# A Mamba, slot and attention block on one core: ScalarE takes the SiLUs at unit 40 in place of 42, z first, and the opening is laid out anew

## The reference

```
h = layernorm(x); xc, z = split(h @ in_w.T)            # 512 channels each
xc = silu(causal_conv4(xc) + conv_b)
dt, B, C = split(xc @ xp_w.T)                          # 16, 16, 16
dt = softplus(dt @ dtp_w.T + dtp_b)
state = exp(dt * A) * state + dt * xc * B              # 512 x 16 states, a scan over tokens
y = (sum over 16 states of state * C + xc * D) * silu(z)
x = x + y @ out_w.T
```

## Time and profile before

| | us |
|---|---|
| median of 3 runs (lowest to highest) | 2333.46 (2328.74 to 2335.32) |
| the profiled execution | 2333.48 |
| its span in the trace | 2331.7 |
| end of the last VectorE instruction of the Mamba in the trace | 1755.4 |

### The profile page before, as it was taken

The page is one execution under the profiler, slowest core; times in us unless marked ns, Lnnn a source line. Parts: engine busy times, 40 slices in busy tenths (PEclk is TensorE's granted clock), DMA queues, the critical chain, the costliest instruction groups (busy, mean ns, idle before and its releaser), DMA issues. The chain is left out here.

```text
span 2331.7 us, 40782 instructions
## 1 busy us (share of the span) xinstructions
PE 2067.5 (89%) x14787; PEld 1241.9 (53%) x14787; DVE 1880.3 (81%) x2584; ACT 1795.9 (77%) x3062; POOL 1654.9 (71%) x1448
## 2 busy tenths in 40 slices
PE   5989898998989898989989898989874879999987
PEld 2445455454545455554545454554533557777765
DVE  6788889898988889898988888888988656666655
ACT  3988998989898988989888989989864434455453
POOL 2789889898989889898989898898995253223110
PEclk9999999999999999999999999999996889999998
DMA  7340505142341515142331405041415000000012
GB/s 243 72 114 23 128 13 124 47 100 67 70 108 29 123 54 128 38 117 56 82 96 41 114 23 128 19 118 40 107 55 179 1 10 20 11 15 16 11 40 73
DMA packets 112237, 166.45 MB, mean 71 GB/s; under 512 B 13219, under 2 KB 58531, under 8 KB 111653
## 3 DMA queue, kind: packets, MB, share of 16 engines
q1 hardware_dynamic: 112036, 163.86, 26.8%
HBM read 125.53 MB, written 34.08 MB: 68 GB/s over the span
## 5 line engine op out<-in xcount | busy, mean ns | idle before, releaser
L640 POOL TENSOR_TENSOR h<-h,C_rep 128x512 f32<-128x512 f32 x1021 | 1270.5, 1277 | 196.3 <-ACT h_carry L549 196.3
L415 DVE TENSOR_TENSOR_SCAN h<-decay,h_carry,psum 128x512 f32<-128x512 f32 x768 | 955.7, 1270 | 126.5 <-PE psum L771 93.8
L541 ACT ACTIVATE decay<-dt_rep,A 128x512 f32<-128x512 f32 x1024 | 729.4, 713 | 96.6 <-DVE h L415 93.3
L771 PE MATMUL psum<-ident,u_B 128*128 128x128 f32 x2048 | 322.0, 282 | 125.1 <-DVE h L415 98.2
L771 PEld LDWEIGHTS psum<-ident,u_B 128*128 128x128 f32 x2048 | 235.2, 141 | 310.4 <-DVE h L415 215.2
L771 PEld LDWEIGHTS psum<-ident,k_r 128*128 128x128 f32 x2048 | 243.3, 142 | 248.8 <-issue 124.7
L415 DVE TENSOR_TENSOR_SCAN h<-decay,zero,psum 128x512 f32<-128x512 f32 x256 | 318.8, 1271 | 50.2 <-PE psum L771 34.7
L771 PE MATMUL psum<-ident,k_r 128*128 128x128 f32 x2048 | 309.9, 279 | 14.2 <-DVE h L415 9.0
L563 ACT ACTIVATE u_B<-u_tok,B_tok 128x512 f32<-128x512 f32 x416 | 295.1, 709 | 35.3 <-PE psum L771 35.3
L563 ACT ACTIVATE k_r<-u_tok,B_tok 128x512 f32<-128x512 f32 x416 | 294.4, 710 | 28.9 <-DVE u_tok L385 17.7
L784 PE MATMUL psum<-h,state_sum 128*32 128x512 f32 x2048 | 279.8, 619 | 3.6 <-POOL h L640 3.4
(11 more groups left out here) (238 smaller groups left out, 2877.2 us busy)
## 6 DMA issues: line engine op xcount, KB each, us to landing
dt_rep<-dt_rows SPq DMA_DIRECT2D x256, 256.0 KB, 5.5
C_rep<-C_rows SPq DMA_DIRECT2D x256, 64.0 KB, 2.0
dt_rows<-x_dt_gated SPq DMA_DIRECT2D x32, 512.0 KB, 4.9
residual<-mamba_residual SPq DMA_DIRECT2D x16, 512.0 KB, 4.0
mamba_residual<-residual SPq DMA_DIRECT2D x16, 512.0 KB, 2.9
x_tok<-mamba_residual SPq DMA_DIRECT2D x15, 512.0 KB, 4.4
f_gru_weights<-in_slot_gru_dram SPq DMA_DIRECT2D x2, 2176.0 KB
u_B<-in_x_dram SPq DMA_DIRECT2D x8, 512.0 KB, 9.1
```

The source lines that it names most:

```text
L415: dve.tensor_tensor_scan(h[:, slot(u)], dec[:, u % DEC], PS[:, u % 2], first, ALU.mult, ALU.add)\
L541: act.activation(dec[:, u % DEC], dtr[:, k % EG], ACT.Exp, scale=A[:, s // STEPS, k:k + 1]).then_inc(S["decay"], 1)
L640: pool.tensor_tensor(h[:, slot(u)], h[:, slot(u)], crep[:, k // EG], ALU.mult).then_inc(S["hc"], 1)
L771: ins = pe.transpose(PS[:, u % 2, tb * P:(tb + 1) * P], pr[f % 2][:, tb, eg], ident[:])
```

## The change

Three things change in `mamba`.

First, ScalarE's SiLUs stand at unit 40 in place of 42 in every step (`A_SILU`, `A_HALO`). Inside, z comes first, then the four SiLUs of x, each waiting for its own convolution in place of all four, then the halo, which came first before. The two exp and two product instructions of units 41 and 42 so stand behind the SiLUs.

Second, in the opening the transposes of x no longer wait for softplus. They go to four PSUM banks of their own (2 to 5), those of dt to four others (0, 1, 6, 7), and the projection to bank 4. DVE copies the four x tiles in a row, then takes the four multiplications.

Third, in the opening four of the first 16 products (2, 6, 10, 14) move from ScalarE to DVE (`first_product`). ScalarE keeps 9. The counts of `prod_a` are lower by four from there on.

```diff
 D_XT = (46, 47, 50, 54)
 D_U = (46, 48, 51, 57)
 A_Z = (5, 6, 9, 15)
-A_SILU = 42
-A_HALO = 42
+A_SILU = 40
+A_HALO = 40
...
+ON_DVE = (2, 6, 10, 14)
+PV = len(ON_DVE)
...
+        xp_bank = lambda p: PA_ if p else CT
+        xt_bank = lambda p, tb: PB_ if p else YB + tb
+        dtt_bank = lambda p, tb: PA_ if p else (0, 1, PA_, PB_)[tb]
...
+                def first_product(j):
+
+                    tb, n = j // SG, j % SG
+                    at(dve, "uT", tb + 1)
+                    at(dve, "bt", 1)
+                    dve.tensor_scalar(pr[0][:, tb, :, EW * n:EW * (n + 1)], uT[:, tb].rearrange("p (g e) -> p g e", e=EW),
+                                      BT[:, 0, tb, n:n + 1], None, ALU.mult).then_inc(S["prod_v"], 1)
...
                 def silus(s):
-                    if s + 1 < ALL:
-                        at(act, "conv", CT * (s + 2))
-                        for ct in range(CT):
-                            act.activation(xc[:, ct], xc[:, ct], ACT.Silu, bias=kc(s + 1, K_CB, ct)).then_inc(S["silu"], 1)
                     if s >= 0:
                         at(act, "z_ev", CT * (s + 1))
                         act.activation(sz[:], sz[:], ACT.Silu).then_inc(S["sz"], 1)
+                    if s + 1 < ALL:
+                        for ct in range(CT):
+                            at(act, "conv", CT * (s + 1) + ct + 1)
+                            act.activation(xc[:, ct], xc[:, ct], ACT.Silu, bias=kc(s + 1, K_CB, ct)).then_inc(S["silu"], 1)
...
+                        if s < ALL and k == A_SILU:
+                            silus(s)
                         if k == A_HALO and p < ALL:
                             halo(p)
-                        if s < ALL and k == A_SILU:
-                            silus(s)
...
                 def tok_x(p, tb):
-                    if tb == 0:
+                    if p == 0:
+                        at(pe, "silu", CT)
+                        at(pe, "conv", CT)
+                        at(pe, "x_ev", CT)
+                    elif tb == 0:
                         at(pe, "dt", 3 * (p + 1))
                     else:
                         at(pe, "xcT", TB * p + tb)
...
                     if eg == 0:
-                        at(pe, "prod_a", PA * (f + 1))
+                        at(pe, "prod_a", PA * (f + 1) - PV)
+                        if f == 0:
+                            at(pe, "prod_v", PV)
                         at(pe, "prod_p", PP * (f + 1))
...
+                        if p == 0 and k == P_XT[0]:
+                            for n in range(TB):
+                                tok_x(p, n)
+                            for n in range(TB):
+                                tok_dt(p, n)
```

More of the change, by code:

```diff
@@ L190, in mamba @@
                  "x_ev conv_mm conv halo xp_mm dbl silu z_mm z_ev sz dt_mm dt_raw dt bt_mm bt xcT_mm xcT dtT_mm uT skip_mm decay "
-                 "b scan carry hc hc_v ysum prod_a prod_p gated o_mm res").split()
+                 "b scan carry hc hc_v ysum prod_a prod_p prod_v gated o_mm res").split()
         S = {n: sem(n) for n in names}
@@ L369, in tok_B @@
                     at(dve, "bt_mm", p + 1)
-                    at(dve, "prod_a", PA * NG * (p - 1))
+                    at(dve, "prod_a", PA * NG * (p - 1) - PV)
                     at(dve, "prod_p", PP * NG * (p - 1))
@@ L377, in tok_x @@
                     if p:
-                        at(dve, "prod_a", PA * (NG * p - 1) + AFTER_A[tb])
+                        at(dve, "prod_a", PA * (NG * p - 1) + AFTER_A[tb] - PV)
                         at(dve, "prod_p", PP * (NG * p - 1) + AFTER_P[tb])
-                    dve.tensor_copy(uT[:, tb], PS[:, PB_]).then_inc(S["xcT"], 1)
+                    dve.tensor_copy(uT[:, tb], PS[:, xt_bank(p, tb)]).then_inc(S["xcT"], 1)
                 def tok_u(p, tb):
@@ L463, in _ @@
                             tok_B(p)
+                        if p == 0 and k == D_XT[0]:
+                            for n in range(TB):
+                                tok_x(p, n)
+                            for n in range(TB):
+                                tok_u(p, n)
+                            for j in ON_DVE:
+                                first_product(j)
                         for n in range(len(D_XT)):
-                            if k == D_XT[n]:
+                            if p and k == D_XT[n]:
                                 tok_x(p, n)
                         for n in range(len(D_U)):
-                            if k == D_U[n]:
+                            if p and k == D_U[n]:
                                 tok_u(p, n)
@@ L525, in projected @@
                     at(act, "bt_mm", p)
-                    act.activation(dbl[:], PS[0:XW, PA_], ACT.Copy).then_inc(S["dbl"], 1)
+                    act.activation(dbl[:], PS[0:XW, xp_bank(p)], ACT.Copy).then_inc(S["dbl"], 1)
                 def softplus(p):
@@ L574, in _ @@
                         f, j = s * NG + k // EG + 1, k % EG
-                        if 0 <= f < ALL * NG and j not in ON_POOL:
+                        if 0 <= f < ALL * NG and j not in ON_POOL and (f or j not in ON_DVE):
                             product(f, j)
@@ L723, in project_dt_B_C @@
                     at(pe, "silu", CT * p + ct + 1)
-                    ins = pe.matmul(PS[0:XW, PA_], WP[:, ct], xc[:, ct], start=(ct == 0), stop=(ct == CT - 1))
+                    ins = pe.matmul(PS[0:XW, xp_bank(p)], WP[:, ct], xc[:, ct], start=(ct == 0), stop=(ct == CT - 1))
                     if ct == CT - 1:
@@ L750, in tok_x @@
                     for ct in range(CT):
-                        ins = pe.transpose(PS[:, PB_, ct * P:(ct + 1) * P], xc[:, ct, tb * P:(tb + 1) * P], ident[:])
+                        ins = pe.transpose(PS[:, xt_bank(p, tb), ct * P:(ct + 1) * P], xc[:, ct, tb * P:(tb + 1) * P], ident[:])
                     ins.then_inc(S["xcT_mm"], 1)
@@ L756, in tok_dt @@
                         at(pe, "dt", 3 * (p + 1))
-                    else:
+                    elif p:
                         at(pe, "uT", TB * p + tb)
                     for ct in range(CT):
-                        ins = pe.transpose(PS[:, PA_, ct * P:(ct + 1) * P], dt[:, ct, tb * P:(tb + 1) * P], ident[:])
+                        ins = pe.transpose(PS[:, dtt_bank(p, tb), ct * P:(ct + 1) * P], dt[:, ct, tb * P:(tb + 1) * P], ident[:])
                     ins.then_inc(S["dtT_mm"], 1)
@@ L870, in _ @@
                                 raw_dt(p, n)
+                        if p == 0 and k == P_XT[0]:
+                            for n in range(TB):
+                                tok_x(p, n)
+                            for n in range(TB):
+                                tok_dt(p, n)
                         for n in range(len(P_XT)):
-                            if k == P_XT[n]:
+                            if p and k == P_XT[n]:
                                 tok_x(p, n)
                         for n in range(len(P_DTT)):
-                            if k == P_DTT[n]:
+                            if p and k == P_DTT[n]:
                                 tok_dt(p, n)
```

2 lines of the change are left out of this document (1 added, 1 removed).

## The result

| | median us (lowest to highest) | runs |
|---|---|---|
| before | 2335.02 (2328.74 to 2335.32) | 5 |
| changed | 2313.82 (2309.66 to 2317.96) | 5 |
| ratio, 95% interval | 0.9923 (0.9908 to 0.9938) | |

The change made the kernel 0.8% faster. (The ratio is the one on record, from all single runs; the quotient of the two medians is 0.9909.) The profiled execution took 2313.48 with a span of 2311.7, so 20.0 less than the one of before. The page of the profile hardly shows it: the shares of the earlier trace rows are the same to a point.

A forecast was written before the change was run, and what follows sets the result against it. No engine was taken as full; the largest wait was VectorE's at each step's SiLUs, with ScalarE the source. Opening 4.2 and 3.0 kept of the steps' 12.7: 2333.48 - 4.2 - 3.0 = 2326.3 us, range 2315 to 2330.5.

The forecast's parts named there:

- The hole: VectorE's wait around the SiLUs in each step; shortened by 0.85 us a turn, nominally 12.7 in 15 steps.
- ScalarE's two waits: ScalarE's waits for a scan (0.49) and the last convolution (some 0.2), filled by z; copy 0.89 us earlier.
- VectorE's new wait for decay 41: Ahead of scan 41 in each step, VectorE waits 2.1 us for ScalarE's decay, where there was no wait.
- The beat: Clock drops on a rhythm outside the kernel hold the mean turn; 3 of the 12.7 us kept, bounds 0 and 12.7.
- a held mean: Mean turn stays at 105.81 us, so some 13 of 15 turns get a clock drop and the 12.7 are given back.
- The rival of the free beat: Turns step over the clock-drop place, as many drops as before, all 12.7 us kept: 2316.6 (2313 to 2320); chance 0.24.
- step 2: The claim on clock drops in the turns: long ones near 106.0 us in most steps, 3 of 12.7 kept.
- The opening: Before the steps: earlier projection, first u and first decay, then chunk 1's rows landing by DMA; 4.2 us gained, bounds 3.4 to 5.4.
- The rival that the hole would stay: Decay 41 comes so late that its scan decides; only the opening gains: 2329.3 (2328 to 2331); chance 0.10.
- the slower one: VectorE reaches its wait at the SiLUs with fewer decays in hand, each turn loses 1.1 us: 2345.8; chance 0.04.

The follow-up runs named there:

- filled kernels: Kernels before and changed, each with idle matmuls added on TensorE at both places where the clock drops: medians 2326.97 and 2310.56 us.
- e3: Changed kernel, but in the steps the old order at unit 40: halo, x once all four convolutions are there, then z; 2388.84 us, single execution.
- e4: Changed kernel with its new order (z, x, halo), but at unit 42 in the steps; 2343.31 us, single execution.
- e1: Kernel before with the new SiLU order at unit 40 in the steps alone, opening as before; 2319.19 us, ratio 0.9940.
- e8: Changed kernel with the load of chunk 1's rows issued earlier, behind the first copies of C; 2316.84 us, ratio 0.9928.
- e11: Changed kernel, but the opening's first 16 products as before, 13 on ScalarE and none on VectorE; 2311.3 us, single execution.
- e7: Kernel before with two idle matmuls a unit in units 59 to 62, filling one of two clock-drop places; 2332.43 us, single execution.
- e5: Changed kernel with z's SiLU in four instructions, one per 128 channels; 2327.57 us, ratio 0.9973.
- e12: Changed kernel with the early load of chunk 1's rows and seven idle matmuls a turn; 2311.42 us, ratio 0.9903.

## Why the prediction was right, and where it was not

Faster, at 0.52 the likeliest of the three, came true. The time, 2313.8, lies 1.2 below the range of 2315 to 2330.5, and 12.5 below the forecast of 2326.3. (The forecast started from 2333.46; by the ratio, 0.9923 of that is 2315.5, just inside the range.) By the two traces, 7.2 was forecast and 20.0 measured. The 12.8 between them are 13.1 too little for the steps, 1.6 too much for the opening, and 1.3 behind the Mamba.

1. **The hole: right, almost to the tenth.** 0.85 a turn was taken, 0.91 measured in the trace (11.79 to 10.88), and 0.91 again between the filled kernels. Load, z, four SiLUs, halo, load, and the copy came in the order and at the distances that were added up. The prediction calls the gain "just ScalarE's two waits", and their rows, 0.49 and some 0.2, make 0.7. Counted from start to start the first is 0.6 (441.51 - 440.31 = 1.20, where such a pair takes 0.61 without a wait), so the two make 0.8, and the last 0.1 lies in how the instructions of the new order overlap. VectorE's new wait for decay 41 was put at 2.1 and is 2.03. The price of each edit alone (e3: 2.4, e4: 0.3) shows why the sum had to be made over both.

2. **The beat: this is the step that failed.** It took "3 of the 12.7 as kept", because 13 turns before had a mean of 105.81. In the trace all of it was kept (15 holes by 0.905, 13.6), and on top the drops cost less: before, four at 1.47 and one turn with both places at 2.44, 8.3 in all; after, 0.90, 0.96, 2.44 and 1.45, 5.8. That makes 16.1 against 3. Nor is that one lucky execution alone: the four unfilled traces with the new steps (the change, e1, e8, e11) have 4, 5, 6 and 5 caught turns of 14, where a held mean asks for some 12. The rival of the free beat, 2316.6, had the mechanism right: a turn that slips by 1.30 steps over the place. e1 shows the two things side by side, groups of caught turns and eight free ones in a row.
 What was wrong in the reasoning was to read a mean as a force. A mean of 105.81 follows if each turn is short enough to slip and is caught whenever it reaches the place; it says nothing of how wide the place is. The prediction wrote that down ("the hold is not tight") and priced it near the other end. The hold does exist, though: e7 has a mean of 105.82 with one place left, e3 has turns of 109.28 in series (so 105.8 is not the only length at which turns can be held), and e5 lost much of its gain with free turns of 104.71. Which of these a new turn length falls into the trace of before did not tell. The prediction's test, "few long ones would refute step 2", was the right one.
 The Trainium skill's rule in "TensorE: Matmul & The Clock Gate" (Part 1), that the block which sets the clock runs freely, agrees with e7: one place filled, the turns caught are others, and the mean is still the 105.8 of before.

3. **The opening: the direction right, the size not.** 4.2 was summed. By chunk 1's copy of B it is 2.94 + 0.55 less the 0.91 of step 0's hole: 2.6; by the opening alone, ratio 0.9984, 3.7; by the filled pair's traces 3.3. That the trace of the change has less than the 3.46 of the opening alone (129.94 against 133.40) goes with the clock, though nothing was run on it: TensorE is at 0.50 from 73.6 to 80.4 in the one, and in the other it is back at 1.00 by 78. The projection came at 37.82, not 37.4 (the convolutions of the earlier trace rows end at 32.27 + 5.32 = 37.59, which the prediction read as about 37.4), ScalarE's products ended at 55.7, not 55.3: the sum of ScalarE's and VectorE's work was good to 0.4. What it left out was dt's way through DRAM: the first decay was put at 56.6, straight behind ScalarE's work, and waits for its DMA to 57.94, and the decay at 76.21 waits 2.29 more. The rows of chunk 1 were issued at 58.46, not the 57.6 of the sum, and landed 12.3 behind that in place of 11.8, so the statistics came at 70.75, not 69.4. The products on VectorE, costed with 2.45 of gain, hid behind the same DMA: e11.

4. **The end.** "Behind the Mamba nothing changes": it was 1.30 shorter in the trace. That was not taken apart, and it is small beside the 7.0 by which that part differs among the 14 traces.

The rival that the hole would stay and the slower one are both refuted by the same rows: scan 42 follows scan 41 after 0.27, and ScalarE reaches unit 40 at the same distance in every turn, free turns being alike to 0.05.

## What to carry to other kernels

When an engine waits around fixed work, put work of its own that has no input to wait for in front, but price the new order and the new place together: here each alone was a loss (0.3 and 2.4 a turn), and both together a gain of 0.9. Where the turns of a loop come in two or three discrete lengths, read the granted clock in short stretches before pricing a gain, and run before and after with a few idle matmuls at the thin places, which tells the gain of the code from the luck of the beat. In an opening with a round trip through DRAM, work taken off the engines is worth only what the DMA leaves. And where a part that the change hardly touches differs by more between executions than the gain, as the part behind the Mamba does here, compare the changed part by marks in the trace.

## What the runs showed of the hardware that was not expected

- TensorE's clock fell behind stretches in which PE waited about half of the time, in pieces of 0.5 to 1.1 us only: PE was busy for 1.50 and 1.40 of the 3.00 us ahead of two drops. The same stretch in other turns has 1.53 and 1.41 and no drop follows. While the clock is down PE's records are full (3.00 of 3.00 in the earlier trace rows): four transposes take 1.11 there and 0.66 just before.
- Seven added matmuls in a turn of 104.46 us kept the clock at 2.4 GHz in all 14 turns of the one trace, at no cost in time.
- Two places in a turn can drop the clock, and when one is filled the other is caught more often: e7's mean of 105.82 is that of before. The fill paid only when both places had it.
- The same kernel varies from execution to execution: before from 2326.61 to 2336.03 in 17 runs of one series, and from 2325.92 to 2329.29 in 10 with the drops filled away. The beat has a part in it, since the fill changes little else (0.15 a turn); but e12, without a drop in its turns, still has 5.3 between its four runs.
- A drop does not cost the same everywhere: 1.4 to 1.5 at the change of steps, 0.9 to 1.0 at the other place, for stretches at 1.2 GHz of the same length. Why was not tried.
- A load of 512 KB issued ahead of dt's small store and loads moved the first decay from 57.94 to 60.33. SP's issue of it takes 0.38, so the rest of the 2.39 is most likely the transfers beside each other; no run shows that. The load itself landed 5.0 us behind its issue there, and 11.8 to 12.5 in before, the change and e11, where it is issued among the copies of dt.
